# Moving a router's work into and beside the last attention layer of a two-layer gated cross-attention kernel

## The reference, cut to what matters

```
# layer 1 attention: q, qx, k, v from fp8-rounded normalized rows, kx, vx from the context
x = x + g_xattn[1] * proj(fp8(concat(attn(q, k, v), attn(qx, kx, vx))))
# layer 1 feed-forward: 8 experts, each token goes to 2 of them
u      = layernorm(x)                       # (16*128, 256)
logits = u @ Wr.T                           # (2048, 8)
top2   = the two largest logits, their softmax as shares
y      = sum over the two e of share_e * (silu(u @ Win[e].T) @ Wout[e].T)
x = x + g_ffn[1] * y
```

## Time and profile before

| what | us |
|---|---|
| median of 3 runs | 1432.77 (1430.90 to 1433.47) |
| the profiled execution | 1431.25 |
| its span | 1429.2 |
| PE busy in the span | 1286.4 (90%) |
| DVE, ACT, POOL busy | 1042.2, 919.3, 756.5 |

### The profile page before, as it was taken

How to read it: one execution, slowest core, us unless ns; L and a number is a source line. 1 busy time by engine, 2 the same in 40 slices (tenths; PEclk the granted TensorE clock), 3 DMA queues, 4 the chain that set the end, 5 groups by cost and what they waited for, 6 DMA issues and landing times. The chain is left out here.

```text
span 1429.2 us, 29957 instructions
## 1 busy us (share of the span) xinstructions
PE 1286.4 (90%) x8831; PEld 949.3 (66%) x8847; DVE 1042.2 (73%) x2336; ACT 919.3 (64%) x3577; POOL 756.5 (53%) x1068
## 2 busy tenths in 40 slices
PE   3899999999988999999999999999999983369991
PEld 2344444444446888888888888888888863359991
DVE  6466666666686888888888888888888777835554
ACT  1345454545577988888888888888888843323330
POOL 2455555545455555666666666666555533823331
PEclk8799999999998999999999999999999995579996
DMA  6443333332132011110111001110120006322225
GB/s 143 104 78 54 72 54 72 54 70 53 40 111 82 2 38 37 37 37 0 37 37 37 21 16 37 37 37 1 38 72 1 1 1 211 122 77 81 83 75 176
DMA packets 134339, 83.50 MB, mean 58 GB/s; under 512 B 67309, under 2 KB 129774, under 8 KB 134256
## 3 DMA queue, kind: packets, MB, share of 16 engines
q1 hardware_dynamic: 125280, 72.50, 20.0%
q0 software_dynamic: 3744, 8.43, 1.6%
q10 hardware_dynamic: 5232, 1.54, 0.5%
HBM read 50.01 MB, written 34.00 MB: 59 GB/s over the span
## 5 line engine op out<-in xcount | busy, mean ns | idle before, releaser
L1422 POOL TENSOR_TENSOR head_rstd<-head_rstd,minus_half 128x4 f32<-128x4 f32 x192 | 239.0, 1245 | 15.1
L1410 ACT ACTIVATE squares<-ps 128x128 bf16<-128x128 f32 x768 | 201.2, 281 | 49.8 <-PE ps L1378 39.8
L1378 PE MATMUL ps<-l_wb,xq 128*128 128x512 f16 (+1 forms) x1024 | 209.9, 328 | 1.2 <-ACT headsT L1446 1.2
L1502 POOL TENSOR_TENSOR prob<-prob,rinv 128x512 f32<-128x512 f32 x128 | 135.2, 1056 | 115.7 <-DVE rinv L1497 114.2
L1489 ACT ACTIVATE prob<-ps,nmax 128x128 f32<-128x128 f32 x512 | 182.4, 383 | 11.8 <-DVE nmax L1480 11.7
L1446 ACT ACTIVATE headsT<-ps,l_hln 128x256 f32<-128x256 f32 (+1 forms) x256 | 166.0, 675 | 29.5 <-PE ps L1437 29.5
L1410 ACT ACTIVATION_READ_ACCUMULATOR squares<-ps 128x1 f32 x768 | 163.0, 212 | 0.0
L1430 DVE TENSOR_TENSOR heads_n<-ps,head_rstd 128x512 f32<-128x512 f32 x192 | 131.4, 684 | 27.9 <-POOL head_rstd L1422 27.8
L702 DVE TENSOR_REDUCE nmax<-ps 128x4 f32<-128x512 f32 x128 | 84.9, 683 | 72.7 <-PE ps L695 72.5
L1473 PE MATMUL ps<-headsT 128*128 128x128 f32 x1024 | 135.1, 275 | 0.0
L1378 PEld LDWEIGHTS ps<-l_wb,xq 128*128 (+1 forms) x1024 | 100.8, 98 | 47.4 <-issue 2.5
(11 more groups left out here) (303 smaller groups left out, 2763.9 us busy)
## 6 DMA issues: line engine op xcount, KB each, us to landing
slots<-blank_slot SPq DMA_DIRECT2D x16, 1161.0 KB, 5.7
taken<-slots SPq DMA_DIRECT2D x23, 258.0 KB
w_out_raw<-in_wprojT SPq DMA_DIRECT2D x8, 512.0 KB, 3.9
raw<-in_winT SPq DMA_DIRECT2D x4, 1024.0 KB, 8.0
raw<-in_woutT SPq DMA_DIRECT2D x4, 1024.0 KB, 5.7
back<-picked SPq DMA_DIRECT2D x8, 512.0 KB, 8.8
q_stack<-q_parts SPq DMA_DIRECT2D x48, 64.0 KB
k_blocks<-k_parts SPq DMA_DIRECT2D x192, 16.0 KB
```

What stands on the lines that cost most here:

```text
L1378: last = e.matmul(out, xq[:, k, which, slot_at], weights(k, hl, c0, n), start=(k == 0 and hl == 0), stop=(k == KD - 1 and hl == 1))
L1410: last = e.activation(squares[:, 4 * n + h, :], A[n][:, h * HD1:(h + 1) * HD1], ACT.Square, scale=HD1**-0.5, accum_out=hss[:, 4 * n + h:4 ...
L1422: e.tensor_tensor(hr[:, four], hr[:, four], t["half"][:, four], ALU.pow).then_inc(g_r[n].sem, 1)
L1502: e.tensor_tensor(prob[:, kind, :, :], prob[:, kind, :, :], spread(rinv[:, kind, :], P), ALU.mult).then_inc(g_p[kind].sem, 1)
```

## The change

- Rows, statistics and packets become steps of layer 1's rounds: `GS`, `GN`, `GO` on DVE, `GR` on POOL, `GH` on ACT, each once for each block, one or two blocks behind the attention.
- Both blocks of instructions after layer 1 and the clearing between them go. The routing's other steps stand in one sequence with layer 1's unrolled end, by a new order of letters, `CLOSING`: `a` is a step of layer 1, `b` one for the logits (`GT` transpose, `GU` copy, `GL` matmuls of one block) or a constant, `d` one of the choice (`GX` copy of logits, `GC` choice in three parts, `GK` ranks, `GA` addresses, `GZ` scatters, `count`, `gap`, `table`), `c` an expert's weights (`XW`).
- The choice is made in 3 groups, of 6, 8 and 2 blocks. The scatters stay 32 indirect DMAs on POOL.
- The weights come in 16 pieces of 0.5 MB through a ring of 8. The ring and `w_in` lie over layer 1's projection weights, `w_out` over the output projection's: SP's first load waits for the last `A`, ACT's ninth piece for the last `O`.
- Layer 0's semaphores are cleared by POOL before its loop of layer 1; each engine adds to `left` when it leaves layer 0, and waits for `cleared` before the closing sequence.
- Layer 1's loop runs over blocks 2 to 11, block 1 is unrolled. `MIXED` is a new order. Buffers of layer 0 lie in another order, `rowsT_n` lies over `q_part`, and the five flags of `r_c` are one.

The core of the diff:

```diff
@@ one_engine @@
+        alternate(e, owner, between(owner), MIXED[owner])
+
+        e.sem_inc(left, 1)
+        second.emit(e, owner, second.before(owner))
+        if owner == "gpsimd":
+            e.wait_ge(left, 5)
+            e.sem_clear(spent)
+            e.sem_inc(cleared, 1)
         second.repeat(e, owner)
-        second.emit(e, owner, second.after(owner))
+        e.wait_ge(cleared, 1)
+        alternate(e, owner, closing(owner), CLOSING[owner])
@@ ORDER1 @@
-    "vector": "PT:1- SC:0 N:2+ RN@3+++ SC:1 RQ:4@2+ RS@3++++ RQ:3@1+ RQ:0@0+ R:0 RQ:1@0+ O-- QM:0- N:0+ R:1 QM:1- "
-              "PT:0 Q:0- Q:1- Q:2- N:1+ Q:3- Q:4- RQ:2@0+",
+    "vector": "PT:1- SC:0 N:2+ RN@3+++ GN@0-- SC:1 RQ:4@2+ RS@3++++ RQ:3@1+ RQ:0@0+ R:0 RQ:1@0+ O-- QM:0- N:0+ R:1 QM:1- "
+              "GS@2- GO@2-- PT:0 Q:0- Q:1- Q:2- N:1+ Q:3- Q:4- RQ:2@0+",
...
+    @s.piece("GS", "vector")
+    def _(e, b, i):
+        e.wait_ge(v_x.sem, v_x.at(J * b + J - 1))
+        e.wait_ge(v_gn.sem, v_gn.at(b - 1))
+        e.memset(spare[:, :], 0.0)
+        e.bn_stats(m_stats[:, :], of(x, b)).then_inc(v_gs.sem, 1)
+        e.wait_ge(v_gs.sem, v_gs.at(b, 1))
+        e.memset(spare[:, :], 0.0)
+        e.bn_aggr(m_mv[:, :], m_stats[:, :]).then_inc(v_gs.sem, 1)
...
+    @s.piece("GN", "vector")
+        e.tensor_scalar(of(m_rows, b), of(x, b), m_mv[:, 0:1], m_rstd[:, 0:1], ALU.subtract, ALU.mult).then_inc(v_gn.sem, 1)
+    @s.piece("GO", "vector")
+        e.tensor_copy(of(packet, b).bitcast(F32)[:, D:D + 1], t["token"][:, bass.ds(b, 1)])
+        e.tensor_tensor(of(packet, b)[:, D:2 * D], of(m_rows, b), of(packet, b)[:, 0:D], ALU.subtract).then_inc(v_go.sem, 1)
...
+    @s.piece("GL", "tensor")
+    def _(e, b):
+        if b == 0:
+            e.wait_ge(wr_in, 16)
+            e.wait_ge(flags["a_hT"][2].sem, flags["a_hT"][2].at(LAST))
...
+        e.wait_ge(a_gu, b + 1)
+        for k in range(KD):
+            last = e.matmul(L[:, b * NE:(b + 1) * NE], u[:, b % 2, k, :], wr[:, k, :], start=(k == 0), stop=(k == KD - 1))
...
+    @s.piece("GZ", "gpsimd")
+    def _(e, b, which):
+        if b == 0 and which == 0:
+            e.wait_ge(t["filled"], 16 * FILLS)
+        e.wait_ge(v_at, [b0 <= b < b1 for b0, b1 in GROUPS].index(True) + 1)
+        e.wait_ge(flags["v_go"].sem, flags["v_go"].at(b))
+        e.indirect_dma_start(
...
+    @s.piece("XW", "scalar")
+    def _(e, n):
+        parting.wait_load(e, n)
+        if n == NE:
+            e.wait_ge(flags["pe_out"].sem, flags["pe_out"].at(LAST))
+        parting.high_part(e, n)
```

More of the change, by code:

```diff
@@ L141, in repeat, with own, alternate, layers @@
             self.emit(e, owner, self.body(owner, i))
-def joined(block, first, second, aside, mixed):
+    def own(self, owner, steps):
+        return [step for step in steps if (step[0], owner) in self.s.pieces]
+def alternate(e, owner, turns, letters):
+    for letter in letters:
+        layer, steps = turns[letter]
+        layer.emit(e, owner, [steps.pop(0)])
+    assert not any(steps for _, steps in turns.values()), (owner, {letter: len(steps) for letter, (_, steps) in turns.items()})
+def layers(block, first, second, between, closing, left, spent, cleared):
     for owner, hook in (("tensor", block.tensor), ("vector", block.vector), ("scalar", block.scalar),
                         ("gpsimd", block.gpsimd), ("sync", block.sync)):
-        both(owner, hook, first, second, aside, mixed)
-def both(owner, hook, first, second, aside, mixed):
+        one_engine(owner, hook, first, second, between, closing, left, spent, cleared)
+def one_engine(owner, hook, first, second, between, closing, left, spent, cleared):
     @hook
@@ L1088 @@
 EXPONENT = 0x7F80
+XW_RING = 8
 FILLS = B
@@ L2143, in program, with between, closing @@
     t = common_tiles(nc)
+    kept = ExitStack()
+    layer1_tiles(nc, t, kept)
     t["filled"] = nc.alloc_semaphore("slots_filled")
-    low = nc.alloc_semaphore("layers_first").num
+    low = nc.alloc_semaphore("layer0_first").num
     with ExitStack() as ctx:
-        layer1_tiles(nc, t, ctx)
         first, bank, places, final, small = layer0(nc, a, t, ctx)
-        second, aside = layer1_attention(nc, a, t, ctx, bank, places, final, small)
-        with nc.Block() as block:
-            joined(block, first, second, aside, MIXED)
-        spent = range(low, nc.alloc_semaphore("layers_last").num + 1)
-        with nc.Block() as block:
-            @block.gpsimd
-            def _(e):
-                e.sem_clear(spent)
-        nc.extend_free_semaphores(list(spent))
+        spent = range(low, nc.alloc_semaphore("layer0_last").num + 1)
+        second, filling, aside, flags, A, S, m_rows, packet = layer1_attention(nc, a, t, ctx, bank, places, final, small)
+        left, cleared = nc.alloc_semaphore("left_layer0"), nc.alloc_semaphore("layer0_cleared")
+        nc.extend_free_semaphores(list(spent))
+        rows, choice, weights = routing(nc, a, t, second.s, flags, A, S, places, m_rows, packet)
+        def between(owner):
+            return {"a": (first, first.own(owner, first.after(owner))), "b": (second, second.own(owner, filling(owner))),
+                    "c": (second, list(aside(owner)))}
+        def closing(owner):
+            return {"a": (second, second.own(owner, second.after(owner))), "b": (second, rows[owner]),
+                    "d": (second, choice[owner]), "c": (second, weights[owner])}
+        with nc.Block() as block:
+            layers(block, first, second, between, closing, left, spent, cleared)
     with ExitStack() as ctx:
         layer1_experts(nc, a, t, out, ctx)
+    kept.close()
 def hadamard(n):
```

633 lines of the change are left out of this document (332 added, 301 removed), and 4 rows, old and new, of the table ORDER1.

## The result

The changed kernel takes 1413.4 us (median of 4 executions, 1412.25 to 1414.34) against 1432.19 (4 executions, 1430.9 to 1433.47) for the one before: a ratio of 0.9876, with a 95% interval of 0.9863 to 0.9888. The forecast was 1417, 15.8 us under the median of 1432.77 that the kernel before had then; the gain came out as 18.8. The profiled execution took 1413.05 us, with a span of 1411.3.

What follows compares the result with a forecast made beforehand. The hole after layer 1, ended by 32 queued scatters on POOL, was taken as the bound. From the profiled 1431.25 us, less 16.9 (scatters), plus 1.0 (loop), gives 1415.4; 1.5 for the median gives 1417, range 1408 to 1426.

Steps and rivals of the forecast that it cites:

- First scatter: Drain of layer 1: first scatter at 1188.5 us, against 1206.28 before, nearer the full-clock end of the addresses' 1185.7 to 1194.
- GR15: POOL's queue: block 15's inverse root behind two scatters costs 0.9 us at full clock, some 2.5 at half; 1.5 taken.
- Scatters beside VectorE: Scatter queue: 14 weight steps on DVE, 16.4 us, hold the scatters 9.3 us in all; bounds 0 and 16.4.
- the price of 0.57 us of delay for one of VectorE: Old kernel's scatters: 7.8 us of extra length over 13.7 us of DVE weight steps beside them, applied to the new steps.
- Loop: Layer 1's loop: added row and statistics steps cost 1.0 us for some 14 blocks; bounds -1 and 24.
- It just fits: Layer 1's loop: the next N becomes 0.47 us late, ends about 841.7, and PE takes it at 841.89.
- Passage: Between the layers: new orders with one wait and POOL's clearing; 0 us taken, with 3 us to either side.
- the sum of -15.9 us: Whole kernel: 16.9 us gained by an earlier end of the scatters, 1.0 us lost in the loop.
- Scatters held in full: Scatter queue: half clock before the logits and DVE's steps paid whole, 1431; either alone 1424; 16 in 100 for one or both.
- Loop loses: Layer 1's loop: PE loses 0.5 us in each of 14 blocks, giving 1423; 9 in 100.
- Slower: Layer 1's loop: inserted DVE work not covered, 1.7 us per block, giving 1440; 4 in 100.
- The choice waiting for the drain's end: Drain: the choice waits as GK0 stands near O(63), and SP's loads set the end, giving 1434; 2 in 100.

Runs made afterwards that it cites:

- e2: Changed kernel with TensorE's transposition of the picks six operations earlier, VectorE's weight part no. 1 behind the first offsets, last round's clearing behind four scatters: 1411.14 us.
- e3: Changed kernel with all of layer 1's drain placed ahead of routing, scatters and experts' weights in every engine's closing order: 1427.96 us, ratio 0.9975.
- e7: Changed kernel with weight item 5 earlier, picks' transposition and TensorE's last-round output six earlier, weight part no. 1 behind the first offsets, clearing behind two scatters: 1406.7 us.
- e4: Changed kernel without VectorE's low weight parts from the third item on, each replaced by a two-column clearing (output wrong): single execution 1409.09 us.
- e5b: Second execution of the changed kernel with one-input VectorE operations in place of low weight parts from the third item on (output wrong): 1408.67 us.
- e10: Changed kernel with one-input operations replacing only VectorE's low parts of the last eight weight items (output wrong): single execution 1411.36 us.
- e6: Changed kernel with the statistics over the new rows taken twice on VectorE, 0.42 us more for each of 16 blocks: 1417.24 us, ratio 0.9902.
- e5: Changed kernel with one-input VectorE operations in place of low weight parts from the third item on (output wrong): first execution 1422.57 us, second 1408.67.

## Why the prediction was right, and where it was off

*First scatter.* Forecast at 1188.5, measured from round 61's add: 23.29 us, where the forecast's numbers give 1188.5 less 1165.44 = 23.06. The mechanism (TensorE is last, not VectorE, and the clock decides) shows in the rows. Everything in the drain is 3.45 us later than the forecast's times, by the start (0.61) and round 61's add (2.84). Less that, VectorE has the picks at 1182.0 and catq at 1182.6, where 1182.4 and 1183.1 were forecast; GK0 ends at 1186.2, between the forecast's 1184.3 and 1192.7 but much nearer the first, although the clock fell in the middle of the logits; the addresses are there at 1187.6, between 1185.7 and 1194. The first scatter starts 1.1 us behind them, in the changed kernel as in e2:

```profile
1190.88 0.17 DVE L1899 CAST r_at_u<-r_at 128x12 uint32<-128x12 f32 x1
```

That 1.1 us is in no term of the forecast. So 1188.5 was near by luck: a value about 1 us too late for the addresses, and nothing for the step from them to the scatter. e2 and e3 show that this term carries the gain.

*GR15.* Forecast 1.5 us, measured 1.0: the next scatter starts at 1195.88 instead of 1.28 behind 1193.70, which is 0.9 later, and takes 0.07 more; no wait. It is the forecast's "only its own 0.9". e7 shows what it costs when O(63) comes too late for it.

*Scatters beside VectorE.* The mechanism was right, as e4, e5b and e10 show (up to what in the low part does it); the size was off. Forecast 9.3 us, measured 4.9. The step that failed is the price of 0.57 us of delay for one of VectorE, taken from steps of 2.29 us. A scatter pays only for the rest of the step under which it begins, so the price hangs on how they meet. In the train of eight a scatter begins 0.1 us into every second step and takes 1.97 us, 1.0 more than alone, for each 2.27 us of VectorE, or 0.44; four of them are 4.0 us. The six steps before it cost 0 to 0.34 each, because a scatter was already running when they began or they were nearly over when one began. The Trainium skill (SBUF — State Buffer, "Who interferes with whom") says that `tensor_reduce` on trn2 never contends with GpSimd; e5b and e10 agree (984 and 1016 ns for a mean scatter, against 1137). Its rule of a full block for the second to issue fits a scatter begun under a step (0.99 us more with 1.11 left), and not as a sum: all 14 steps paid whole would have been 16.4 us.

*Loop.* Forecast 1.0 us, measured 0.0 from round 3 to round 56. The forecast's picture is in the trace (timeline of VectorE and of TensorE, changed kernel):

```profile
841.15 0.42 DVE L1640 BATCH_NORM_STATS2 r_m_stats<-x_rows 128x6 f32 x1
...
842.06 0.42 DVE L1668 TENSOR_TENSOR r_packet<-r_m_rows,r_packet  x1
842.41 0.68 DVE L1556 COPY probT<-ps 128x512 f32<-128x512 f32 x1
...
844.28 0.68 DVE L1468 TENSOR_TENSOR heads_n<-ps,head_rstd 128x512 f32<-128x512 f32 x1
...
845.09 0.60 PE L1475 MATMUL ps<-ident,heads_n 128*128 128x128 f32 x4
```

Everything here is 3.20 us later than before, by the shift of the passage. Less that, `heads_n` starts at 841.08, 0.53 late where 0.47 was forecast, without its wait, and TensorE takes it at 841.89, to the hundredth as before. "It just fits", by 0.1 to 0.2: e6 says 0.12.

*Passage.* Forecast 0, with 3 to either side; measured 2.6 us of loss. Inside the range, but by luck, as the difference of 5.2 gained and 7.7 lost. The forecast gave no working for it, only "no row prices an order". One could have followed the buffer: the last load takes the place of an earlier item, so it waits for that item's low part, and in VectorE's new order that letter stands far back.

So the sum of -15.9 us became -18.7 at the last scatter: passage +2.6, loop -0.7, first scatter +0.2, scatters -4.9 (51.6 less 46.7, of which holding 4.4). A loss and a gain that the forecast didn't have, the passage's and the scatters', cancel in part. Of the 3.6 us between 1417 and 1413.4 another 1.2 are the step from the profiled execution to the median: 1.5 was taken from the kernel before, and it was 0.35 (1413.40 less 1413.05). The rest, from the last scatter's end to TensorE's start and the experts, is unchanged within 0.2 us, as said.

*Rivals.* Scatters held in full: no. Loop loses: its place was real and 0.12 us away. Slower: no. The choice waiting for the drain's end: a part of it was true of one matmul, GK0, which stood 4 us behind its picks; e2 took most of that back.

## What to carry to other kernels

Where a load's buffer is freed by another engine's step in a hand-written order, the load's real place is that of the freeing letter; look it up for each letter that a new order moves, since a late one costs several engines at once (7.7 us here). A long VectorE operation like these low parts (two SBUF inputs) beside a queue of indirect DMAs is paid partly by that queue: each DMA issued while one runs waits for its rest. Keep such operations off that stretch, or look whether a form with one input exists. Count how often an inserted step runs before pricing it: per block and per round differ by four here. Before trusting a gain of 2 us from two profiles, take off what the executions differ by at an event that no edit touches.

## What the runs showed of the hardware

*The clock fell though TensorE was busy.* In the changed kernel it was granted 1.00 in 1170 to 1180 with 9.45 us busy, and 0.63 in 1180 to 1190 with 9.57 us busy; the fall, from 2.4 to 1.2 GHz (1.00 in 1181 to 1182, 0.50 in 1183 to 1184), is at 1182.5, in a row of 128x8 and 128x128 matmuls without gaps over 0.1 us since 1181.1, which themselves follow a full loop. A share of busy time did not tell it beforehand.

*A stretch of slow dispatch.* In the first execution of e5 VectorE's small operations of the addresses and the table came mostly 1.40 us apart (0.7 to 2.9) from 1209 to 1239 us, where they come 0.2 apart elsewhere:

```profile
1233.64 0.18 DVE L1948 SCALAR_TENSOR_TENSOR spot<-nth,spot 128x24 f32<-128x24 f32 x1 [1.01 <-DVE spot L1947]
1235.04 0.17 DVE L1949 CAST shelf_row<-spot 1x24 int32<-1x24 f32 x1 [1.22 <-issue]
...
1237.84 0.18 DVE L1951 TENSOR_SCALAR tile_owner<-tile_owner 128x24 f32<-128x24 f32 x1 [2.54 <-remote]
```

It began beside the scatters and went on behind the last of them, which was issued by 1234.9, so they alone can't cause it; the waits are put down to "issue", to "remote" (a releaser that the profile names no further) or to VectorE's own previous step. The same kernel a second time, on another chip, shows none of it, nor do the other kernels that ran on the first chip. The cause stays open. What it teaches is that a single execution can carry 14 us that don't come again, and that such a run has to be read from the rows asked about: here the scatters, which were the same in both (31.5 us in e5b, and none but the first over 1.1 us in either).
